# Two side steps of a hand-planned timeline stand later: the queries' transposes of group 0 and the statistics of the first routing

## The chip, the cores and the metric

The kernel runs on one core of one Trainium2 chip. The metric is the device time of one execution in microseconds (us), median over the runs. All arithmetic is in 32-bit floats.

## What is computed

The input is 16 sequences ("batches" here) of 512 tokens by 128 features. Each goes through six stages, each with a residual; `_L0_ffn_ref`, `_L0_attn_ref` and so on are plain functions of the reference:

```python
x = x + 0.5 * _L0_ffn_ref(_layernorm(x), W, b, V_r, C)          # one 128x128 product with a low-rank correction
x = x + _L0_attn_ref(_layernorm(x), ...)                        # 16 heads of 8; state = q; twice: state = softmax(state k^T) v
x = x + 0.5 * _L0_ffn_ref(_layernorm(x), W, b, V_r, C)          # the same first-kind FFN once more
x = x + 0.5 * _L1_ffn_ref(_layernorm(x), gate_w, w1, w2, w3, w1s, w2s, w3s)   # 8 experts, top 2, and a shared one
x = x + _L1_attn_ref(_layernorm(x), ...)                        # 16 heads of 8, masked softmax attention
x = x + 0.5 * _L1_ffn_ref(_layernorm(x), ...)                   # the experts once more, same weights
```

In the first attention q and k are divided by their norms per head before use. In the expert stage `softmax(x gate_w^T)` gives scores, the best two experts of each token are taken, and each does `silu(x w1) * (x w3)`, then `w2`.

## The kernel before, in words

Every engine plays a list of steps that a planner in the same file, class `Timeline` (from L107), has put in order before the program is built. `timeline()` (L277) gives each step a position in **slots** (one slot is one pair of score matmuls, about 2.1 us); a steady batch takes 96 slots (TURN), and work of about four batches is interleaved. `Timeline.close()` (L121) goes through the slots and places each step at the later of its due position and, where it has `behind=(other, gap)`, the place of the other step plus the gap. Steps in SIDE_EVENTS also need room in the slot's TensorE load (COST; FULL 1.0 for the fillers m_gu and m_down, OVER 1.4 for others) and one of three PSUM "side banks"; what finds none waits for the next slot. Then each engine gets its own list, sorted by place plus a lag of that step on that engine (LAG, L97 to L105; the lag of a step that is not listed is 0):

```python
self.order = {e: sorted(numbered, key=lambda m: (m[0] + lag.get(m[2], 0), m[1])) for e, lag in LAG.items()}
```

`play()` (L512) issues each engine's list in that order. A step waits by semaphores for what it needs, and what stands behind it on its engine waits too. The places set the order only, not a time.

The steps that matter here, b being the batch:

- **st(kind, b, g, i)**, L678: two score matmuls (32 rows by 512) of head group g (four heads) into the two banks B_ST; it waits until ScalarE's exponential (L820) of the st before has read them. Kind S1 and S2 are the first and second step of the first attention, L1 is the second attention. Eight st make one window of a group, and ScalarE's exponential writes probs.
- **pv(kind, b, g, kc)**, L693: the products of probs with the values, eight records in the trace. ScalarE or VectorE then copies the result to uts (L832, L1039).
- **sm(kind, b, g, half, tc)**, L714: two score matmuls the other way round (L726), into one pair of banks B_SM, which VectorE reduces to the row maxima (L1072). Each sm waits for the reduction of the one before.
- **p0_op(b, g, i)**, L669: turns the operands of the first attention for head group g, four transposes at L589: i = 0 the keys (stack0k), i = 1 the queries (stack0q). It waits for GpSimd's `low_parts` (L1245: a subtraction at L1248 and a copy at L1250). ScalarE copies the result to kT or qT (L785; in the lag table 1.2 for p0_op, 0.8 for st). The window S1 of group 0 of that batch starts some 8 slots later.
- **ffn_y(b, k)**, L638, the product of the first-kind FFN; k = 1 is the second FFN. VectorE adds it to the tokens in two halves (ffn_y and ffn_rest, both at L951), waits for itself and then raises ffn_done at L961.
- **m_stats(b, k)**, L1090: VectorE's statistics (L920) for the layer norm ahead of the experts; k = 0 is the first of the two expert stages ("routing"). **m_aggr** (L1094): four aggregates (L927) and two small operations (L932, L913), then on GpSimd twelve small operations, Newton's steps for the inverse root (L1177 to L1182; lag 0.6 on GpSimd). **m_xt** (L737): four transposes of the tokens (L589), which wait for ffn_done; ScalarE copies them to xT_m (L785). **m_logits** (L741, VectorE L1097 to L1106): the gate product; on VectorE it waits first for Newton's steps.
- **m_xe(b, k, e)**, L1302 (L1310) on GpSimd: the input of expert e; from the third on it waits until TensorE has done the second half of m_gu for expert e - 2. **m_gu(b, k, e, h)**, L754 (L761) on TensorE: the two products of an expert for half the tokens; ScalarE's tanh (L850) and VectorE's two operations (m_gu L1135, m_up L1141) finish them. At the place of the change, in batch b's first routing, the experts of batch b - 3's second stage are under way.

Of the kernel before, what the change touches and what calls it, by code (L numbers as in the profile page):

```python
# [218 lines left out]
def window(t, start, kind, b, g):  # L219
    for i in range(WIN):  # L220
        t.at(start + i, "st", kind, b, g, i)
    for kc in range(TC):
        t.at(start + 2 * kc + PV_AT, "pv", kind, b, g, kc)
    t.at(start + 10.2, "uts", kind, b, g)
    if kind == "S1":
        t.at(start + DIVIDE_AT, "divide", b, g)
        t.at(start + STATE_AT, "state", b, g)
    else:
        t.at(start + 11.2, "turn", kind, b, g)


def max_job(t, start, kind, b, g):
    seen = [0, 0]
    for slot in SM_AT:

        half = (start + slot + 1) % 2
        t.at(start + slot + 0.01, "sm", kind, b, g, half, seen[half])
        seen[half] += 1
    t.at(start + JOB + 0.6, "mx", kind, b, g)
    t.at(start + JOB + 1.2, "rows", kind, b, g)  # L240


def ffn_events(t, start, b, k):
    t.at(start, "ffn_stats", b, k, behind=(("o_y", b, 0), 1) if k else None)
    t.at(start + 1, "ffn_aggr", b, k, behind=(("ffn_stats", b, k), 1))
    t.at(start + 1.4, "ffn_xt", b, k, behind=(("ffn_stats", b, k), 0.2))
    t.at(start + 2.4, "ffn_bias", b, k, behind=(("ffn_xt", b, k), 0.8))
    t.at(start + 4.2, "ffn_y", b, k, behind=(("ffn_xt", b, k), 1.6))
    t.at(start + 5.2, "ffn_rest", b, k, behind=(("ffn_y", b, k), 1))


def moe_events(t, start, units, unit, b, k):

    t.at(start, "m_stats", b, k, behind=(("o_y", b, 1), 1) if k else (("ffn_y", b, 1), 2))
    t.at(start + 1, "m_aggr", b, k, behind=(("m_stats", b, k), 1))
    t.at(start + 1.4, "m_xt", b, k, behind=(("m_stats", b, k), 0.2))
    t.at(start + 3.8, "m_logits", b, k, behind=(("m_xt", b, k), 1.8))
    t.at(start + 5.2, "m_probs", b, k, behind=(("m_logits", b, k), 1.2))
    t.at(start + 6.6, "m_index", b, k, behind=(("m_probs", b, k), 0.9))
    t.at(start + 6.6 + 1, "m_pick", b, k, behind=(("m_index", b, k), 1))  # L260
    t.at(start + 9.2, "m_gt", b, k, behind=(("m_pick", b, k), 1.3))
    for e in range(EX):
        t.at(units + 2 * unit * e - 2, "m_xe", b, k, e, 
             behind=(("m_gu", b, k, e - 2, 1), 0.8) if e >= 2 else (("m_gt", b, k), 3.5))
        for h in range(2):
            t.at(units + unit * (2 * e + h) + 0.5, "m_gu", b, k, e, h,
                 behind=(("m_xe", b, k, e), 1.2) if h == 0 else (("m_gu", b, k, e, 0), 0.4))
            t.at(units + unit * (2 * e + h) + 0.5 + UP_BEHIND, "m_up", b, k, e, h, behind=(("m_gu", b, k, e, h), UP_BEHIND))
    last = ("m_gu", b, k, NE, 1), 2.2
    for tc in range(TC):  # L270
        for part in range(2):
            t.at(units + 2 * unit * EX + 1.4 + 2 * tc + part, "m_down", b, k, tc, part, behind=last)
            last = ("m_down", b, k, tc, part), 0.4
    return units + 2 * unit * EX + 10


def timeline():  # L277
    t = Timeline()
    for i, at in enumerate(FOLD_AT):
        t.at(at, "fold", i)  # L280
    t.at(MASKS_AT, "masks")
    for b in range(NB):
        t0, t1, t2, t3 = STARTS[b:b + 4]
        early, last = b < EARLY, b == NB - 1
        t.at(t0 - 60 if b else FOLD_AT[0], "load", b, behind=(("store", b - NX), 0.1) if b >= NX else None)
        ffn_events(t, t0 + FFN0_AT, b, 0)
        p = t0 + P0_AT
        t.at(p, "p0_stats", b, behind=(("ffn_y", b, 0), 2))
        t.at(p + 1, "p0_aggr", b, behind=(("p0_stats", b), 1))
        t.at(p + 1.4, "p0_xt", b, behind=(("p0_stats", b), 0.2))  # L290
        t.at(p + 4, "p0_res", b, behind=(("p0_xt", b), 1.4))
        for tc in range(TC):
            t.at(p + 4.6 + tc, "p0_qkv", b, tc, behind=(("p0_xt", b), 2.4))
        t.at(p + 9.4, "p0_squares", b, behind=(("p0_qkv", b, TC - 1), 1.4))
        t.at(p + 11.5, "p0_sums", b, behind=(("p0_squares", b), 1.8))
        for i in range(2):
            t.at(p + 17 + i, "p0_hi", b, i, behind=(("p0_sums", b), 5 + i))
        for g, at in enumerate(P0_OP_AT):
            for i in range(2):
                t.at(t0 + at + i + 0.4, "p0_op", b, g, i, behind=(("p0_hi", b, i), 2.4))  # L300
        for g in range(NG):
            window(t, t0 + (EARLY_S1_AT if early else S1_AT)[g], "S1", b, g)
            window(t, t0 + (EARLY_S2_AT if early else S2_AT)[g], "S2", b, g)
            max_job(t, t0 + (EARLY_MAX_AT if early else S2_MAX_AT)[g], "S2", b, g)
            at = L1_END[b][g] if b in L1_END else t2 + L1_AT[g]
            window(t, at, "L1", b, g)
            max_job(t, at - L1_MAX_END if b in L1_END else t2 + L1_MAX_AT[g], "L1", b, g)
        o = t1 + O0_AT
        t.at(o + 0.4, "o_t", b, 0, behind=(("turn", "S2", b, NG - 1), 1.2))
        t.at(o + 1.9, "o_y", b, 0, behind=(("o_t", b, 0), 1.4))  # L310
        ffn_events(t, o + 3.2, b, 1)
        units, unit, p = (MOE0_END, UNIT_END, P1_END) if last else (t1 + MOE0_AT, UNIT0, t1 + P1_AT)
        if b == 0:
            units, unit, p = t1 + EARLY_MOE0_AT, EARLY_UNIT, t1 + EARLY_P1_AT
        moe_events(t, o + 8.5, units, unit, b, 0)
        done = ("m_down", b, 0, TC - 1, 1), 1.4
        t.at(p, "p1_stats", b, behind=done)
        t.at(p + 1, "p1_aggr", b, behind=(("p1_stats", b), 1))
        t.at(p + 1.4, "p1_xt", b, behind=(("p1_stats", b), 0.2))
        t.at(p + 2.4, "p1_res", b, behind=(("p1_xt", b), 0.8))  # L320
        for tc in range(TC):
            t.at(p + 4.2 + tc, "p1_qkv", b, tc, behind=(("p1_xt", b), 2.4))
        t.at(p + 8, "p1_values", b, behind=(("p1_qkv", b, TC - 1), 0.8))
        for i in range(2):
            t.at(p + 8.2 + i, "p1_hi", b, i, behind=(("p1_qkv", b, TC - 1), 1 + i))
            for n in range(TC):
                t.at(p + 11.4 + 4 * i + n, "p1_op", b, n, i, behind=(("p1_hi", b, i), 3))
        o = OUT1_END.get(b, t2 + O1_AT)
        t.at(o + 0.4, "o_t", b, 1, behind=(("turn", "L1", b, NG - 1), 1.2))
        t.at(o + 1.9, "o_y", b, 1, behind=(("o_t", b, 1), 1.4))  # L330
        units, unit = (MOE1_END[b], UNIT_END) if b in MOE1_END else (t3 + MOE1_AT, UNIT1)
        end = moe_events(t, max(o + 3.2, units - 18), units, unit, b, 1)
        t.at(end, "store", b, behind=(("m_down", b, 1, TC - 1, 1), 1.5))
    return t.close()
# [6 lines left out]
def build(nc, x, ffn_wT, ffn_vT, ffn_cT, ffn_b, wqkv0, bqkv0, wo0, bo0, lnw, lnb,  # L341
          wqkv1, bqkv1, wo1, bo1, src, tgt, gateT, w13, w2, ident, consts, out):
    line = timeline()
    order, no, use = line.order, line.no, line.use
    with ExitStack() as ctx:
# [1018 lines left out]
```

## Time and profile before

| | |
|---|---|
| median of 3 runs | 3438.26 us (3430.40 to 3438.31) |
| profiled execution, its own time | 3441.13 us |
| its span | 3439.3 us |
| mean granted TensorE clock | 0.975 |
| TensorE matmuls busy | 92% of the span |
| VectorE, ScalarE, GpSimd busy | 69%, 60%, 37% |

The rows come from one profiled execution. A busy share is the time in which an engine has an instruction under way. In the timeline a row is one instruction, or several alike that follow each other (x4): its start and length in us, engine, line, operation, what it writes and reads with the shape of each, and in brackets how long the engine had stood still before it and what released it. A matmul in 32-bit floats leaves two records (x8 for pv), one of the scores leaves one. A granted clock of 1.00 is 2.4 GHz, one of 0.50 is 1.2 GHz.

### The profile page before, as it was taken

Reading aid. Unit: us, or ns where it says so; the run is one execution under the profiler, and the core shown is the slowest. Engines: PE = TensorE matmul, PEld = TensorE weight load, DVE = VectorE, ACT = ScalarE, POOL = GpSimd, SP = SyncE. Lnnn points to the kernel's source line nnn. Section 1 sums busy time; section 2 is a strip of 40 time slices with the busy share of each in tenths; the row PEclk is TensorE's granted clock in tenths of the full one; section 3 lists DMA queues with packets and bytes.
Section 4 is the critical chain, followed back from the end, with each engine's and each line's share of the span. In section 5 each row is a group of like instructions: output and inputs, shape, how many; then the busy total and the mean of one; then the engine's idle time right before and its main releaser. Section 6 shows DMA issues by size and latency. Waiting matters only on the chain.

```text
span 3439.3 us, 55298 instructions
## 1 busy us (share of the span) xinstructions
PE 3175.8 (92%) x19942; PEld 1653.5 (48%) x19942; DVE 2360.7 (69%) x5153; ACT 2078.9 (60%) x2689; POOL 1267.5 (37%) x2419
## 2 busy tenths in 40 slices
PE   6898999999999999999999999999999999998899
PEld 3444444444544444454444445444444544444557
DVE  3654675867678686767868676786867677676573
ACT  3464566666656666665666666666666656665442
POOL 3324242343435234243523424352343435223321
PEclk8998999999999999999999999999999999999999
DMA  1000001001100010111010011100101111000111
GB/s 42 4 29 4 32 2 32 32 5 35 32 35 31 31 35 5 35 32 35 30 32 26 14 35 33 35 31 31 35 5 35 32 35 32 30 32 4 60 35 35
DMA packets 81502, 96.89 MB, mean 28 GB/s; under 512 B 50544, under 2 KB 68400, under 8 KB 81104
## 3 DMA queue, kind: packets, MB, share of 16 engines
q1 hardware_dynamic: 81232, 93.35, 8.5%
q8 instruction: 162, 2.65, 0.3%
q14 instruction: 108, 0.88, 0.1%
HBM read 82.76 MB, written 4.78 MB: 25 GB/s over the span
## 4 chain that ended last, share of the span: by engine, by line
PE 62%; ACT 15%; DVE 14%; POOL 5%; issue 4%; ACTq 0%; DMA 0%; SPq 0%; DVEq 0%; POOLq 0%
PE ps L689 16%; PE ps L706 14%; ACT probs L820 13%; PE ps L771 8%; PE ps L761 8%; DVE negmax L1072 6%; PE ps L589 5%; PE ps L726 4%; PE ps L595 2%; PE ps L584 2%; PE ps L654 1%; DVE hid L1141 1%; DVE th L1135 1%; DVE uts L1039 1%; DVE X L951 1%
## 5 line engine op out<-in xcount | busy, mean ns | idle before, releaser
L820 ACT ACTIVATE probs<-ps 128x1024 f32<-128x1024 f32 x1536 | 1574.8, 1025 | 1006.6 <-PE ps L689 991.2
L1072 DVE TENSOR_REDUCE negmax<-ps 128x2 f32<-128x1024 f32 x1024 | 1250.5, 1221 | 452.8 <-PE ps L726 434.8
L689 PE MATMUL ps<-qT,kT 32*128 32x512 f32 x3072 | 779.3, 503 | 117.4 <-ACT probs L820 72.4
L706 PE MATMUL ps<-probs,v 128*32 128x512 f32 x6144 | 839.0, 619 | 0.0
L1310 POOL TENSOR_TENSOR xe<-xT_m,G 128x512 f32<-128x512 f32 x288 | 367.6, 1277 | 988.5 <-PE ps L761 943.6
L761 PE MATMUL ps<-xe,w_sb 128*128 128x256 f32 x2304 | 656.9, 410 | 12.9 <-DVE hid L1141 8.8
L689 PEld LDWEIGHTS ps<-qT,kT 32*128 32x128 f32 x3072 | 289.1, 184 | 768.8 <-ACT probs L820 509.4
L726 PE MATMUL ps<-kT,qT 32*128 32x512 f32 x2048 | 521.4, 504 | 55.0 <-DVE negmax L1072 54.6
L761 PEld LDWEIGHTS ps<-xe,w_sb 128*128 128x128 f32 x2304 | 400.2, 193 | 185.6 <-issue 133.1
L1135 DVE SCALAR_TENSOR_TENSOR th<-th,ps 128x256 f32<-128x256 f32 x576 | 236.4, 411 | 187.3 <-ACT th L850 181.8
L850 ACT ACTIVATE th<-ps 128x256 f32<-128x256 f32 x576 | 221.5, 385 | 149.5 <-PE ps L761 135.5
L771 PEld LDWEIGHTS ps<-w_sb,hid 128*128 128x128 f32 x2304 | 270.0, 191 | 74.5 <-issue 68.5
L771 PE MATMUL ps<-w_sb,hid 128*128 128x128 f32 x2304 | 301.8, 282 | 0.8 <-DVE X L1149 0.5
L1287 POOL TENSOR_TENSOR qT<-maxrow,qT 128x512 fp32r<-128x512 f32 x128 | 163.2, 1275 | 319.8 <-DMA maxrow<-negmaxT 319.8
L1141 DVE TENSOR_TENSOR hid<-ps,th 128x256 f32<-128x256 f32 x576 | 242.3, 421 | 15.5
L726 PEld LDWEIGHTS ps<-kT,qT 32*128 32x128 f32 x2048 | 194.6, 184 | 118.2 <-DVE negmax L1072 60.6
L706 PEld LDWEIGHTS ps<-probs,v 128*32 128x32 f32 x6144 | 122.4, 109 | 192.1 <-issue 187.7
L832 ACT ACTIVATE uts<-ps 128x512 f32<-128x512 f32 x128 | 105.3, 823 | 51.9 <-PE ps L706 48.8
L584 PE MATMUL ps<-id_sb 128*128 128x128 f32 x848 | 124.8, 292 | 0.0
L584 PEld LDWEIGHTS ps<-id_sb 128*128 128x128 f32 x848 | 106.6, 197 | 25.2 <-issue 24.7
L1275 POOL CAST qstack<-st 128x256 fp32r<-128x256 f32 x64 | 25.3, 396 | 217.4 <-DVE st L1045 217.4
L589 PEld LDWEIGHTS ps<-id_sb,uts 128*128 128x128 f32 x512 | 53.9, 140 | 94.8 <-issue 94.3
(171 smaller groups left out, 2684.2 us busy)
## 6 DMA issues: line engine op xcount, KB each, us to landing
G<-gates_dram SPq DMA_DIRECT2D x96, 768.0 KB, 6.2
maxrow<-negmaxT SPq DMA_DIRECT2D x512, 2.0 KB
v<-v_tok SPq DMA_DIRECT2D x256, 18.0 KB, 1.9
X<-in_x SPq DMA_DIRECT2D x16, 256.0 KB, 2.8
out<-X SPq DMA_DIRECT2D x16, 256.0 KB, 2.3
w_sb<-in_w SPq DMA_DIRECT2D x1, 1152.0 KB, 7.1
w_sb<-in_w SPq DMA_DIRECT2D x1, 576.0 KB, 8.7
gates_dram<-gT SPq DMA_DIRECT2D x32, 18.0 KB
```

What stands on the lines that cost most here:

```text
L584: nc.tensor.matmul(bank[:, c * P:(c + 1) * P], id_sb[:], id_sb[:], start=True, stop=True)
L589: ins = nc.tensor.transpose(bank[:, i * P:(i + 1) * P], t, id_sb[:])
L689: nc.tensor.matmul(ps[:, B_ST + h, :], kT[a][rows, g * S + kc * P:g * S + (kc + 1) * P], qT[a][rows, g * S:(g + 1) * S], start=True, stop= ...
L706: ins = nc.tensor.matmul(ps[ROWS * j:ROWS * (j + 1), B_UT, :], v[:, at:at + ROWS], probs[:, n % QUADS, j, :], start=(kc == 0), stop=(kc == ...
L726: nc.tensor.matmul(ps[:, B_SM + h, :], qT[a][rows, g * S + tc * P:g * S + (tc + 1) * P], kT[a][rows, g * S:(g + 1) * S], start=True, stop= ...
L761: ins = nc.tensor.matmul(bank[:, HALF * i:HALF * (i + 1)], w13_sb[:, e, i, :], source, start=True, stop=True)
L771: ins = nc.tensor.matmul(side_bank(key)[:, 0:P], hid[:, e, tc * P:(tc + 1) * P], w2_sb[:, e, :], start=(e == 0), stop=(e == EX - 1))
L820: nc.scalar.activation(probs[:, quad % QUADS, j:j + 2, :], ps[:, B_ST:B_ST + 2, :], ACT.Exp).then_inc(sem["exp_done"], 1)
L1072: nc.vector.tensor_reduce(negative[:, tc, 2 * half:2 * half + 2], ps[:, B_SM:B_SM + 2, :], AX_X, ALU.max, negate=True).then_inc(sem["sm_re ...
L1135: nc.vector.scalar_tensor_tensor(out=th[n % 2][:], in0=th[n % 2][:], scalar=1.0, in1=side_bank(key)[:, 0:HALF], op0=ALU.add, op1=ALU.mult) ...
L1141: nc.vector.tensor_tensor(hid[:, e, HALF * h:HALF * (h + 1)], side_bank(key)[:, HALF:S], th[n % 2][:], ALU.mult).then_inc(read_signal(key), 1)
L1310: nc.gpsimd.tensor_tensor(xe[n % 2][:], xT_m[run % 2][:], G[:, e * S:(e + 1) * S], ALU.mult).then_inc(sem["m_xe"], 1)
```

## The change

It changes two numbers of the timeline. In the first routing of each batch (k = 0) m_stats stands at least 2.9 slots behind the second FFN's ffn_y, where it stood 2 behind; m_aggr and m_xt are tied to m_stats. The queries' p0_op of group 0 is due 2 slots later than before; those of the other groups and all keys' stay.

```diff
 def moe_events(t, start, units, unit, b, k):
 
-    t.at(start, "m_stats", b, k, behind=(("o_y", b, 1), 1) if k else (("ffn_y", b, 1), 2))
+    t.at(start, "m_stats", b, k, behind=(("o_y", b, 1), 1) if k else (("ffn_y", b, 1), 2.9))
     t.at(start + 1, "m_aggr", b, k, behind=(("m_stats", b, k), 1))
     t.at(start + 1.4, "m_xt", b, k, behind=(("m_stats", b, k), 0.2))
...
         for g, at in enumerate(P0_OP_AT):
             for i in range(2):
-                t.at(t0 + at + i + 0.4, "p0_op", b, g, i, behind=(("p0_hi", b, i), 2.4))
+                t.at(t0 + at + i + (2.4 if i and g == 0 else 0.4), "p0_op", b, g, i, behind=(("p0_hi", b, i), 2.4))
```

## Rows read from the trace of the kernel before

**Rows 1.** The chain that ended last, by engine, share of the span.
```profile
PE 62%; ACT 15%; DVE 14%; POOL 5%; issue 4%; ACTq 0%; DMA 0%; SPq 0%; DVEq 0%; POOLq 0%
```

**Rows 2.** TensorE's waits: waiting line, what released it, us in total, times, longest.
```profile
PE ps L589 <- DVEq L961: 18.8, 13, 1.5
PE ps L589 <- POOL stack0q L1250: 14.4, 13, 1.2
```

**Rows 3.** Timeline of TensorE around the queries' transposes of batch 8, start and length.
```profile
1515.28 1.07 PE L706 MATMUL ps<-probs,v 128*32 128x512 f32 x8
1517.45 0.66 PE L589 MATMUL ps<-id_sb,stack0q 128*128 128x128 f32 x4 [1.10 <-POOL stack0q L1250]
...
1518.46 1.16 PE L595 MATMUL ps<-wo,xT_b 128*128 128x128 f32 x8
1519.73 0.50 PE L689 MATMUL ps<-qT,kT 32*128 32x512 f32 x2
```

**Rows 4.** Timeline of GpSimd at the same place.
```profile
1516.59 0.81 POOL L1250 COPY stack0q<-stack0q 128x512 f32<-128x512 f32 x1
```

**Rows 5.** Timeline of ScalarE at the same place.
```profile
1515.41 1.02 ACT L820 ACTIVATE probs<-ps 128x1024 f32<-128x1024 f32 x1 [0.24 <-PE ps L689]
...
1519.58 0.59 ACT L785 ACTIVATE qT<-ps 128x512 fp32r<-128x512 f32 x1
...
1521.36 0.60 ACT L832 ACTIVATE uts<-ps 128x512 f32<-128x512 f32 x1
1522.37 1.02 ACT L820 ACTIVATE probs<-ps 128x1024 f32<-128x1024 f32 x1 [0.41 <-PE ps L689]
```

**Rows 6.** Timeline of TensorE around m_xt of batch 9, at full clock.
```profile
1967.13 1.13 PE L761 MATMUL ps<-xe,w_sb 128*128 128x256 f32 x4
1969.70 0.66 PE L589 MATMUL ps<-id_sb,X 128*128 128x128 f32 x4 [1.44 <-DVEq L961]
...
1970.72 1.07 PE L706 MATMUL ps<-probs,v 128*32 128x512 f32 x8
1972.12 0.50 PE L689 MATMUL ps<-qT,kT 32*128 32x512 f32 x2 [0.33 <-ACT probs L820]
...
1972.55 1.13 PE L761 MATMUL ps<-xe,w_sb 128*128 128x256 f32 x4
...
1980.66 0.50 PE L726 MATMUL ps<-kT,qT 32*128 32x512 f32 x2 [0.38 <-DVE negmax L1072]
```

**Rows 7.** Timeline of GpSimd at the same place: Newton's steps, then m_xe.
```profile
1971.51 0.20 POOL L1179 TENSOR_TENSOR m_n<-m_n 128x4 f32<-128x4 f32 x1 [4.34 <-DVE m_n L913]
...
1974.58 0.20 POOL L1182 TENSOR_TENSOR m_n<-m_n 128x4 f32<-128x4 f32 x1
1974.73 1.27 POOL L1310 TENSOR_TENSOR xe<-xT_m,G 128x512 f32<-128x512 f32 x1
```

**Rows 8.** Timeline of VectorE at the same place.
```profile
1968.99 0.60 DVE L951 SCALAR_TENSOR_TENSOR X<-ps,f_n,X 128x128 f32<-128x128 f32 x2
...
1971.79 0.42 DVE L1141 TENSOR_TENSOR hid<-ps,th 128x256 f32<-128x256 f32 x1
1972.72 1.23 DVE L1072 TENSOR_REDUCE negmax<-ps 128x2 f32<-128x1024 f32 x1 [0.51 <-PE ps L726]
...
1976.60 0.19 DVE L1102 TENSOR_TENSOR lg<-ps,m_n 128x32 f32<-128x32 f32 x1 [0.47 <-PE ps L595]
```

**Rows 9.** Stretches of whole rounds: length; busy us (instructions) per engine; granted clock; DMA share; GB/s.
```profile
929.55:1937.41 1007.86, 947.87 (x5961) 479.17 (x5961) 734.38 (x1600) 648.15 (x841) 393.55 (x750) 0.97 0.09 29
1937.41:2933.18 995.77, 934.13 (x5962) 475.66 (x5961) 733.61 (x1600) 647.76 (x841) 393.51 (x750) 0.99 0.09 29
2534.43:2732.82 198.39, 185.70 (x1193) 94.57 (x1192) 146.70 (x320) 129.51 (x169) 78.73 (x150) 1.00 0.09 30
```

## The prediction

> **What bounds the kernel now.** I read the chain of work that ended last first: 62% of the span is TensorE's, and VectorE, ScalarE and GpSimd share most of the rest [rows 1]. So TensorE's instruction stream sets the time; another engine counts only where TensorE stands still for it. The waits of TensorE come second [rows 2]: 13 waits for a result of the FFN (the VectorE semaphore step at L961), 18.8 us, and 13 for the query operands stack0q from GpSimd, 14.4 us. In the timeline twelve of each lie in the steady rounds (a round is one batch, 96 slots, some 200 us): 1.44 us ahead of the transposes of m_xt for batches 3 to 14, and 1.10 us ahead of p0_op(b, 0, 1) for batches 4 to 15. These are the two steps that the diff moves. Then I read the timeline around one of each, on every engine, because a queue is played in a fixed order: a step that moves passes others on TensorE and, by its lag, on ScalarE, VectorE and GpSimd too. Last came the rounds and their granted clock.
>
> **The query operands, second line of the diff.** By the code, p0_op(8, 0, 1) has stood at slot 719.84; its new due time puts it at 720.7, behind st(S2, 7, 3, 0) at 720 and behind o_y(5, 1), ahead of the st at 721. Nothing is added or removed. On ScalarE its copy (lag 1.2) stood at 721.04 and now stands at 721.9, behind the exponential of the st at 721 (lag 0.8, 721.8) and ahead of the uts copy at 722.2. VectorE, GpSimd and SP keep their order: p0_op has no step on them, and the DMAs of the rows are not passed.
>
> Before: TensorE ends pv at 1515.28 + 1.07 = 1516.35 and then waits until GpSimd's copy of stack0q ends at 1516.59 + 0.81 = 1517.40 [rows 3, 4]. After: the st goes as soon as the exponential before it is read, 1515.41 + 1.02 = 1516.43 [rows 5], so at about 1516.48 to 1516.98; o_y takes 1.16 less the overlap of 0.07, to 1518.08; stack0q has been ready since 1517.40, so the four transposes run without a wait, 0.66 less 0.07, to 1518.67. The next st, at 1519.73 before, starts at 1518.60: its exponential (from 1517.1, 1.02 long) is over by 1518.13. That is **1.13 us** less. Its wait of 1.10 is gone and 0.6 us of cover stands ahead of the same copy.
>
> Does something behind it take this back? ScalarE now runs exponential, copy 0.59, uts 0.60 in a row: from 1519.17, ends at about 1520.20, 1520.7 and 1521.2. The next exponential would be ready at 1522.37 - 1.13 = 1521.24 [rows 5]. So the cover is there, but with 0.05 us only. What ScalarE loses there, 0 to 0.59 (one whole copy), is the bound of this cost; I take 0, as the order just fits. The three side banks are handed out anew for o_y and this step; by the code each takes a bank whose reader has been done for at least 1 us. Twelve rounds by 1.13 is **13.6 us**; the bounds are 12 x 0.54 = 6.5 and 13.6. For batches 0 to 3 the step stood where nothing waits behind it, or keeps its order: 0.
>
> **The routing, first line of the diff.** For batch 9 m_stats goes from slot 934.69 to 935.59, m_xt from 934.9 to 935.79: behind the st at 935 and the pv at 935.6. m_aggr is tied to m_stats + 1 and goes to 936.59: on VectorE behind m_up at 936.42, and on GpSimd (lag 0.6, 937.19) behind m_xe for expert 7 at 937.02. On ScalarE the exponential goes ahead of the copy of xT_m. No DMA is passed.
>
> TensorE first. It is free at 1967.13 + 1.13 = 1968.26 and waits until 1969.70 for the second FFN, whose last VectorE row ends at 1968.99 + 0.60 = 1969.59 [rows 6, 8]. Now st and pv (0.50 and 1.07 less overlaps) fill 1968.2 to 1969.7, m_xt comes at 1969.7 as before, and the next st and sm start at 1970.3 in place of 1972.12: 1.8 us earlier. But the sm behind them waits for VectorE, which has the same work in another order and is through with m_stats, m_gu, m_up and m_aggr at 1971.79 + 0.42 = 1972.21 either way; its reduction then starts 0.5 us earlier than at present, no more. So 1.8 becomes 0.59 by the sm of slot 937.
>
> Then m_logits. VectorE's step waits for the twelve GpSimd instructions of Newton's steps. They ran from 1971.51 to 1974.78, 3.27 us, with 1.8 us to spare before VectorE used them at 1976.60 [rows 7, 8]. Now m_xe stands before them, and m_xe waits for m_gu of expert 5. That ended at 1972.55 + 1.13 = 1973.68 and ends at 1971.85 in the new order; m_xe runs 1.27, so Newton's steps start at 1973.15 and end at 1976.42, and VectorE goes on at 1976.46: **0.14 us** earlier than before. From there VectorE is full to the sm of slot 940, for which TensorE already stands still 0.38 us [rows 6]; TensorE meets it 0.14 us earlier and waits longer. So of 1.44 us removed 0.14 is left, times 12 is **1.7 us**. Bounds: 0, where m_xe ends 0.14 us later than I have it, and 0.59 x 12 = 7.1, where Newton's steps were not late. I take 0.14: it is the sum of measured durations in the order that the code gives. In the trace GpSimd does keep its order: m_xe had its input at 1973.68 and yet started at 1974.73, right behind Newton's last row [rows 6, 7].
>
> The Trainium skill says the same of queues ("Perfetto Trace Analysis", Tensor Engine Instruction: ScalarE, VectorE and GpSimd are strictly first in, first out), and this rule speaks against this part of the change: by it the part gives 1.7 us in all, without it it would give 7.1. The trace agrees with the rule, with the 1.05 us of the row just named.
>
> **The clock.** Ten rounds in a row took 1007.86 + 995.77 = 2003.6 us, mean 200.36; the shortest of them took 198.39, at a granted clock of 1.00 [rows 9]. The first five have 201.57 on average at a mean grant of 0.97: a part of each ran at 1.2 in place of 2.4 GHz, which costs 3.18 us over the shortest round. The other five have 199.15, that is 0.76 over it. So the clock costs 1.97 us a round, and the same work at a given place pays it or not. A round that is 1.27 us shorter need not come back to the same falls each time, which would give up to 1.2 us a round (1.97 less 0.76); against this, the idle time of the routing is not gone but stands later, next to waits that are already there. Bounds: 1.2 x 12 = 14 us of gain, and 15 us of loss, where all twelve rounds are of the long kind (12 x 3.2 = 38 against 12 x 1.97 = 24). I take 4 us of gain, a quarter of the better bound.
>
> **Sum.** 13.6 + 1.7 + 4 = 19.3 us. The profiled execution took 3441.13 (span 3439.3), 2.9 us over the median of the three runs; against it the sum gives 3421.8, against the median of 3438.26 it gives **3419**, which I forecast.
>
> **Rivals.** (1) The routing gives more than I have, 0.59 us or up to 1.44 a round, since Newton's steps are in time or VectorE's slack is larger. For it: 1.8 us of slack before. Against it: the count above. It gives 5 to 15 us more, 3404 to 3414. Chance 0.13. (2) What the query operands give is taken back in ScalarE's row of four, or by the next wait for GpSimd; then 0 to 6 us remain of 13.6, and with the clock's 4 the time is some 3429 to 3434. For it: a cover of only 0.05 us. Chance 0.11. (3) The falls of the clock come in all rounds: 15 us of loss against 15.3 of gain, 3438. Chance 0.10. (4) Slower: the wait of the routing, now moved next to the waits at slots 940 and 941, brings one more fall in each round. One fall cost up to 3.2 / 2 = 1.6 us a round (half of a long round's surplus, an estimate). With all rounds long (15 us) and one more fall in each (19 us) against 15.3 of gain the kernel is 19 us slower, 3457; it decides from the point where rounds lose over 4.1 us each to the clock, against 1.97 now. The five long rounds lost 3.2 on average. Chance 0.06. Beside it the Trainium skill ("TensorE: Matmul & The Clock Gate", What's actually happening) says that the low clock is the default and that activity lifts it; by this rule idle time that is merely moved can move the fall with it. (5) The change doesn't do what it says, since the planner puts the steps back by other rules: worked through in the code it doesn't, chance 0.02. My own case has 0.58.
>
> **Range and chances.** About 0.3%, 10 us, is what a measurement of this kernel can tell from no change. My case with the clock at its two bounds reaches from 3409 to 3438; with part of rival 1 below, 3406, and rival 2 above, 3434, it leaves out most of rivals 3 and 4 and the lower half of 1. Faster by over 0.3%: my case and rival 1 = 0.71; within 0.3%: rivals 2, 3 and 5 = 0.23; slower 0.06.
>
> **What would show it.** Right: no wait of TensorE for stack0q in the rounds; the wait at L961 near 0.1; new waits of TensorE for VectorE of some 0.9 us ahead of the sm of slot 937 and 0.9 ahead of that of slot 940 (0.38 before); GpSimd's m_xe ahead of Newton's steps, and VectorE's m_logits released by them; the shortest round at full clock 197.1 us. Wrong: a shortest round of 198.4 (rival 2) or under 196.7 (rival 1), or a mean granted clock in the rounds under 0.97 (rivals 3 and 4).

## The result, and the profile after

The changed kernel takes **3421.54 us** (median of 8 runs, 3416.62 to 3426.41), the kernel before 3435.85 in the runs beside it. The ratio is 0.9962, 95% interval 0.9946 to 0.9978: 0.38% faster, 13 us by the ratio (7.6 to 18.6). One of the eight executions of the kernel before took 4435.23 us in a slow state; it counts in the median, which is 3433.43 without it, and not in the ratio. The forecast was 3419. The profiled execution took 3423.68 us, span 3421.9, mean granted clock 0.972 (0.975 before).

TensorE's waits, as in [rows 2]. Of the thirteen waits each for L961 and stack0q one of each is left, both in the first 700 us: 1.2 us for stack0q, and for L961

```profile
PE ps L589 <- DVEq L961: 1.6, 1, 1.6
```

Timeline of TensorE at the queries' transposes of batch 8, as in [rows 3]:

```profile
1506.32 1.07 PE L706 MATMUL ps<-probs,v 128*32 128x512 f32 x8
1507.63 0.50 PE L689 MATMUL ps<-qT,kT 32*128 32x512 f32 x2 [0.24 <-ACT probs L820]
1508.06 1.16 PE L595 MATMUL ps<-wo,xT_b 128*128 128x128 f32 x8
1509.05 0.60 PE L589 MATMUL ps<-id_sb,stack0q 128*128 128x128 f32 x4
1509.58 0.50 PE L689 MATMUL ps<-qT,kT 32*128 32x512 f32 x2
```

From the pv to the second st it took 4.45 us (1515.28 to 1519.73) and takes 3.26 (1506.32 to 1509.58). The st, the product and the transposes follow each other with one wait of 0.24 us.

ScalarE at the same place, as in [rows 5]:

```profile
1510.15 1.02 ACT L820 ACTIVATE probs<-ps 128x1024 f32<-128x1024 f32 x1 [0.90 <-PE ps L689]
1511.07 0.59 ACT L785 ACTIVATE qT<-ps 128x512 fp32r<-128x512 f32 x1
1511.55 0.60 ACT L832 ACTIVATE uts<-ps 128x512 f32<-128x512 f32 x1
1512.22 1.03 ACT L820 ACTIVATE probs<-ps 128x1024 f32<-128x1024 f32 x1
```

The row of four is as forecast, and the next exponential starts 0.62 us after the st that it reads (1511.60), as before (1522.37 after 1521.75): the cover just holds.

Timeline of TensorE around m_xt of batch 5, as in [rows 6]. This stretch is at full clock up to 1161.36:

```profile
1154.49 1.06 PE L706 MATMUL ps<-probs,v 128*32 128x512 f32 x8
1155.58 0.66 PE L589 MATMUL ps<-id_sb,X 128*128 128x128 f32 x4
...
1159.14 0.50 PE L726 MATMUL ps<-kT,qT 32*128 32x512 f32 x2 [0.74 <-DVE negmax L1072]
...
1172.42 0.50 PE L726 MATMUL ps<-kT,qT 32*128 32x512 f32 x2 [0.96 <-DVE negmax L1072]
```

Timeline of GpSimd, as in [rows 7]:

```profile
1157.82 1.27 POOL L1310 TENSOR_TENSOR xe<-xT_m,G 128x512 f32<-128x512 f32 x1 [4.78 <-PE ps L761]
1159.05 0.21 POOL L1179 TENSOR_TENSOR m_n<-m_n 128x4 f32<-128x4 f32 x1
...
1162.15 0.20 POOL L1182 TENSOR_TENSOR m_n<-m_n 128x4 f32<-128x4 f32 x1
```

Timeline of VectorE, as in [rows 8]:

```profile
1162.38 0.19 DVE L1102 TENSOR_TENSOR lg<-ps,m_n 128x32 f32<-128x32 f32 x1 [1.11 <-POOL m_n L1182]
```

The reader sees the wait travel. It is gone ahead of m_xt; 0.74 us of it stands ahead of the sm of slot +2 (1159.14), and VectorE then waits 1.11 us for Newton's steps, which stand behind m_xe. At the sm of slot +5 (1172.42) TensorE waits 0.96 us, where it waited 0.38. The forecast had 0.9 at both places. m_logits starts 6.80 us after m_xt, where it was 6.90 (1976.60 less 1969.70): 0.10 us is what is left.

Ten rounds, the first of them (batch 4) and 28.23 us of that round around m_xt; then two stretches, one just ahead of a fall of the clock and one in it. The columns are those of [rows 9]:

```profile
925.68:2918.74 1993.06, 1893.88 (x11922) 962.53 (x11921) 1469.21 (x3200) 1294.14 (x1681) 788.94 (x1500) 0.98 0.09 29
925.68:1123.28 197.60, 188.19 (x1193) 95.67 (x1193) 146.56 (x320) 129.43 (x169) 78.92 (x150) 0.98 0.09 30
950.30:978.53 28.23, 26.00 (x145) 12.34 (x142) 23.99 (x64) 15.54 (x21) 12.85 (x28) 0.88 0.01 2
...
1154.06:1161.36 7.30, 6.37 (x42) 2.94 (x42) 6.33 (x18) 4.26 (x6) 2.88 (x10) 1.00 0.00 0
...
1161.36:1168.19 6.83, 6.83 (x26) 3.00 (x26) 5.28 (x26) 2.81 (x5) 1.59 (x6) 0.50 0.00 0
```

The ten rounds are only 10.6 us shorter (2003.6 before), though the queries alone should give 11.3. The kernel before had rounds at full clock; here **every round from batch 3 to 14 spends 6.8 to 13.7 us in all at the low clock**, and each has a low stretch that begins 5 to 14 us behind m_xt, as the one above at 1161.36, 5.8 us behind it.

What a low stretch costs depends on where it stands. The round above has 6.8 us of it, from 5.4 us behind m_xt on, and takes 197.60 us, only 0.5 us over the 197.1 forecast for full clock. In the kernel before, the round of batch 13 has the same 6.8 us from 14.4 us behind m_xt on and takes 200.36, which is 1.97 over its full-clock round of 198.39. A reading of this, which no run tests by itself: just behind m_xt TensorE would stand still for VectorE anyway, so being slow costs little there.

### The profile page after: what moved, and what is told of

Read it like the earlier page. It is cut to its first block, busy times and chain, and to the rows that moved or that the text cites. A ratio compares the mean times of both kernels' runs of the same rounds, so it can differ in the third digit from the quotient of the medians.

```text
span 3421.9 us, 55298 instructions
## 1 busy us (share of the span) xinstructions
PE 3183.4 (93%) x19942; PEld 1659.5 (48%) x19942; DVE 2362.8 (69%) x5153; ACT 2076.4 (61%) x2689; POOL 1271.0 (37%) x2419
## 4 chain that ended last, share of the span: by engine, by line
PE 62%; ACT 15%; DVE 14%; issue 4%; POOL 4%; ACTq 0%; DMA 0%; SPq 0%; DVEq 0%; POOLq 0%
PE ps L689 16%; PE ps L706 14%; ACT probs L820 13%; PE ps L761 9%; PE ps L771 8%; DVE negmax L1072 6%; PE ps L589 5%; PE ps L726 4%; PE ps L595 2%; PE ps L654 2%; PE ps L584 2%; DVE th L1135 1%; DVE uts L1039 1%; DVE hid L1141 1%; ACT uts L832 1%
```

## The experiments

All times are medians; each ratio is to the kernel before in the same comparison. There the kernel before took 3432.72 us for q_alone to aggr_first, 3433.50 for fill_both to fill_q, 3435.67 for the four fill3 and 3438.83 for fill_xt. A **full-clock round** is the shortest of the rounds of batches 3 to 13 in which the granted clock never fell; the **second eighth** is slots 12 to 24 of such a round, the stretch that holds m_xt and m_logits. The last three columns come from one profiled execution of each kernel, and executions of one kernel differ in their clock (3422.0 us at a mean grant of 0.984 to 3440.9 at 0.975 for the kernel before), so the counts of rounds are rough.

| kernel | us | ratio, 95% interval | full-clock round | its second eighth | rounds without a fall, of 11 |
|---|---|---|---|---|---|
| before | 3435.85 | | 198.39 | 27.73 | 2 |
| both parts (the change) | 3421.54 | 0.9962, 0.9946 to 0.9978 | none | none | 0 |
| q_alone | 3413.64 | 0.9944, 0.9924 to 0.9965 | 197.23 | 27.73 | 2 |
| r_alone | 3438.61 | 1.0020, 1.0006 to 1.0034 | none | none | 0 |
| newton_first | 3406.91 | 0.9928, 0.9909 to 0.9947 | none | none | 0 |
| aggr_first | 3411.33 | 0.9948, 0.9928 to 0.9969 | 196.56 | 27.11 | 1 |
| fill_both | 3410.23 | 0.9935, 0.9917 to 0.9954 | 197.39 | 28.07 | 2 |
| fill_newton | 3402.88 | 0.9911, 0.9895 to 0.9927 | 196.65 | 27.21 | 4 |
| fill_q | 3405.41 | 0.9923, 0.9907 to 0.9939 | 197.00 | 27.73 | 7 |
| fill3_before | 3415.59 | 0.9943, 0.9926 to 0.9960 | 198.14 | 27.72 | 7 |
| fill3_r | 3416.78 | 0.9949, 0.9932 to 0.9966 | 198.13 | 27.63 | 8 |
| fill3_both | 3408.03 | 0.9923, 0.9905 to 0.9941 | 196.82 | 27.61 | 6 |
| fill3_newton | 3409.79 | 0.9921, 0.9903 to 0.9939 | 196.54 | 27.19 | 4 |
| fill_xt | 3404.83 | 0.9913, 0.9892 to 0.9934 | 196.52 | 27.21 | 6 |

### q_alone: the queries' part by itself

```diff
-                t.at(t0 + at + i + 0.4, "p0_op", b, g, i, behind=(("p0_hi", b, i), 2.4))
+                t.at(t0 + at + i + (2.4 if i and g == 0 else 0.4), "p0_op", b, g, i, behind=(("p0_hi", b, i), 2.4))
```

> The queries' part alone. Theory 1 (the two parts add up): the twelve waits for stack0q are gone, a steady round is 1.13 us shorter outside the clock's falls, 13.6 us in all: 3422 us against 3436 before (the medians of eight runs), and the m_xt wait of 1.44 us is still there. Theory 2 (the routing's part costs more through the clock than it gives): this kernel is as fast as the one with both parts, or faster: 3412 to 3421, with falls of the clock no more frequent than before, while the kernel with both parts has 6.8 to 13.7 us at the low clock in every round. Theory 3 (ScalarE's row of four takes it back): 3428 or more.

Measured 3413.64, in theory 2's range. A full-clock round and its second eighth, stretches of the profile:

```profile
2113.33:2310.56 197.23, 185.53 (x1194) 94.63 (x1194) 146.76 (x320) 129.43 (x169) 78.92 (x150) 1.00 0.09 30
2137.95:2165.68 27.73, 23.30 (x145) 11.24 (x141) 24.20 (x64) 15.55 (x21) 12.91 (x28) 1.00 0.01 2
```

The round is 1.16 us shorter than the 198.39 of before [rows 9], against 1.13 forecast, and the second eighth is unchanged. Twelve rounds give 13.9 us; the ratio gives 19 (0.56%). Theory 1 is right on the round, theory 2 on the time. The rest, 5 us, lies within the interval's 7 us either way, so the times do not show that the clock gained anything here. The grants point that way: their mean is 0.983 over the 7 executions, against 0.980 over 18 of the kernel before, where 0.001 of grant went with about 2.1 us (18.9 us over 0.009). Theory 3 is out.

### r_alone: the routing's part by itself

```diff
-    t.at(start, "m_stats", b, k, behind=(("o_y", b, 1), 1) if k else (("ffn_y", b, 1), 2))
+    t.at(start, "m_stats", b, k, behind=(("o_y", b, 1), 1) if k else (("ffn_y", b, 1), 2.9))
```

> The routing's part alone. Theory 1: 0.10 to 0.14 us a round, 1.7 us: 3434 us. Theory 2: the idle time that is moved behind m_xt makes the clock fall in every round in the stretch from 5 to 14 us behind m_xt, which costs more than 0.14: 3436 to 3450, mean granted clock in the rounds 0.965 or less. Outside the falls both expect the same: no wait at m_xt, 0.74 us ahead of the sm of slot +2, m_logits released on VectorE by Newton's last step.

Measured 3438.61, ratio 1.0020, and the interval leaves out 1: **by itself this part makes the kernel slower**, by 7 us, though every wait that it moves is as counted. No round is free of falls, as theory 2 has it; but the mean grant of the rounds is 0.98, not its 0.965 or less. Over all executions the mean grant is 0.973 (12 of them), against 0.980 (18) for the kernel before. In the profile the round of batch 5 takes 198.80 us, with 6.8 us at the low clock from 5.4 us behind m_xt on, and those with 10.2 us take 200.5 to 201.4. The two ratios multiply to 0.9964, and the change has 0.9962: the parts add up.

### newton_first and aggr_first: who takes the routing's gain

newton_first changes GpSimd's order alone, in the steady rounds; aggr_first puts m_aggr back on VectorE as well, so that against the kernel before only TensorE's and ScalarE's order is changed at this place.

```diff
# newton_first, on top of the change
-             "rows": 2 * HOP, "divide": 1.0},
+             "rows": 2 * HOP, "divide": 1.0, "m_aggr": 0.4},
```

```diff
# aggr_first, on top of the change
-    t.at(start + 1, "m_aggr", b, k, behind=(("m_stats", b, k), 1))
+    t.at(start + (1 if k else 0), "m_aggr", b, k, behind=(("m_stats", b, k), 1 if k else 0.2))
```

> Both parts, and on GpSimd alone m_aggr's Newton steps stand ahead of m_xe again (lag 0.4 in place of 0.6). If m_xe ahead of them is what holds the routing's gain down to 0.1 us (theory 1), VectorE's m_logits starts some 0.45 us earlier behind m_xt than with both parts, released by TensorE's product (at 6.3 to 6.4 us behind m_xt instead of 6.8), and the kernel is 5.4 us faster than with both parts: 3416. If VectorE is full anyway (rival), m_logits comes earlier but the sm of slot +5 does not, and the time stays at 3421.

> Both parts, with m_aggr right behind m_stats on VectorE as in the kernel before, and so Newton's steps ahead of m_xe on GpSimd too. Theory 1: the same gain as with the lag alone, 3416, since VectorE has the same work up to the next reduction either way. Rival: the order on VectorE is what counts, and this one is faster or slower than the other by over 3 us.

VectorE's first step of m_logits and TensorE's m_xt in newton_first, batch 5, two timelines:

```profile
1158.48 0.19 DVE L1102 TENSOR_TENSOR lg<-ps,m_n 128x32 f32<-128x32 f32 x1 [0.49 <-PE ps L595]
```

```profile
1152.30 0.66 PE L589 MATMUL ps<-id_sb,X 128*128 128x128 f32 x4
```

The step comes 6.18 us behind m_xt and is released by TensorE's product, no longer by Newton's steps. The second eighth at full clock in aggr_first:

```profile
747.44:774.55 27.11, 23.47 (x144) 11.21 (x141) 24.09 (x64) 15.47 (x21) 12.82 (x28) 1.00 0.01 2
```

It is 0.62 us shorter than the 27.73 of before, where the forecast's bound without the queue was 0.59. So TensorE's part of the move is worth 0.6 us a round, and the order on VectorE and GpSimd takes 0.5 of it. The order on GpSimd alone takes 0.4, by the full-clock stretches of fill_newton and fill3_newton below (27.21 and 27.19, against 27.61 of fill3_both). The times went further than the 3416 expected of both: newton_first by 9 us. Its rounds have 5.1 us at the low clock on average, those of the change 9.5. aggr_first is 4.4 us slower than newton_first, over the 3 us of the rival, but the intervals overlap, so a difference by VectorE's order is not shown.

### fill_both, fill_newton, fill_q: extra products that hold the clock

To set the clock apart I gave TensorE redundant work just where it waits; FILL lists the experts and halves.

```diff
+FILL = ((4, 0), (5, 1), (6, 0), (6, 1))
...
                 source = xe[(EX * run + e) % 2][:, HALF * h:HALF * (h + 1)]
+                if k == 1 and b < 12 and (e, h) in FILL:
+                    nc.tensor.matmul(bank[:, 0:HALF], w13_sb[:, e, 0, :], source, start=True, stop=True)
                 for i in range(2):
```

In fill_q, on top of q_alone, (5, 0) stands in place of (5, 1); fill_newton is on top of newton_first.

> Both parts, and in rounds 3 to 14 four extra products of 0.5 us on TensorE (m_gu's first product twice, the first one overwritten), right ahead of the longest waits for VectorE's reductions. If the moved idle time makes the clock fall (theory 2), the falls go, the granted clock in the steady rounds is 0.99 or more, and a round takes 197.1 to 197.5 us: 2 us a round less than the 199.3 of both parts, 3395 to 3402. If the falls have another cause, the clock stays at 0.97 and the four products make the kernel as slow as with both parts or up to 24 us slower: 3421 to 3445.

> The same four products with Newton's steps ahead of m_xe. Without falls a round takes 198.4 - 1.13 - 0.6 = 196.7 us against 197.1 to 197.5 with both parts and the products: the worth of the GpSimd order, free of the clock, is 0.5 us a round, 6 us, and the kernel takes 3390 to 3396. If VectorE is full anyway (rival), it is the same as the kernel with both parts and the products.

> The queries' part alone with four such products (one of them ahead of the m_xt wait of 1.44 us in place of the wait behind it). Without falls a round takes 197.3 us: against the kernel with both parts and the products this gives the routing's part free of the clock, 0.10 us a round or 1.2 us, so 3397 to 3403. If the routing's part lost time by something else than the clock, this kernel is 5 us or more faster than that one.

fill_both missed its time: 3410, not 3395 to 3402. The falls became shorter, 2.7 us a round on average against 9.5, but only two rounds had none. And it carried a cost that I had not counted. GpSimd and VectorE in fill_both behind m_xt of batch 10, which began at 2142.50:

```profile
2145.17 1.27 POOL L1313 TENSOR_TENSOR xe<-xT_m,G 128x512 f32<-128x512 f32 x1 [5.20 <-PE ps L764]
```

```profile
2149.73 0.19 DVE L1105 TENSOR_TENSOR lg<-ps,m_n 128x32 f32<-128x32 f32 x1 [1.54 <-POOL m_n L1185]
```

The product in expert 5 comes ahead of the one for which m_xe waits: m_xe starts 2.67 us behind m_xt (2.24 in the change) and m_logits 7.23 (6.80), both 0.43 later, and the second eighth is 28.07 in place of 27.61. This is the chain m_gu, m_xe, Newton, m_logits seen from the other side: it passes a delay on in full. fill_newton, where the chain is cut, has 27.21 with the same products. It is 7 us faster than fill_both, though the intervals overlap, and its 3403 missed the 3390 to 3396; it too has falls left, in 7 rounds of 11. fill_q's 3405 missed 3397 to 3403. It is 5 us faster than fill_both, which its expectation takes for a sign that the routing loses by something else than the clock; but fill_both's delay of 0.43 us in twelve rounds is 5 us too, so these three do not price the routing by themselves.

### fill3: the same without the product in expert 5

> The kernel before, with three of the extra products (experts 4 first half, 6 both halves; none in the half that m_xe and Newton's steps wait for). It is the ground for the next two. Theory 2: the extra products keep the clock up, so it is as fast as the kernel before or a few us faster though it does more, 3425 to 3436, and a round free of falls takes 198.4 as before. Rival: 0.5 us for each product, 10 to 20 us slower.

> The routing's part alone, with the same three products. A round free of falls takes 198.3 us against 198.4 in the one before: the part gives 0.10 us a round when the clock is left out. Theory 2 (its loss is the clock's): the ratio of this kernel to the kernel before with the products lies under that of the two without products (1.002), at 0.998 to 1.001. Rival (it loses by a wait): rounds free of falls are longer than 198.4.

> Both parts with the three products: rounds free of falls take 197.15 us (the four products took 197.4, since one of them delayed m_xe and with it Newton's steps), and the second eighth of the round 27.63 us against 27.73 before. Time 3403 to 3412. If the product in expert 5 was not what delayed that one, the second eighth stays at 28.07.

> Both parts, Newton's steps ahead of m_xe, three products. Rounds free of falls take 196.6 us, the second eighth 27.1 to 27.2: 0.5 us a round better than fill3_both, 6 us: 3397 to 3405, the fastest so far. If VectorE were full anyway, it would equal fill3_both.

FILL is ((4, 0), (6, 0), (6, 1)) on top of the kernel before, r_alone, the change and newton_first. Second eighths at full clock, fill3_before, then fill3_r:

```profile
1940.00:1967.72 27.72, 24.09 (x148) 12.00 (x145) 24.18 (x64) 15.64 (x21) 12.85 (x28) 1.00 0.01 2
```

```profile
1346.84:1374.47 27.63, 24.37 (x148) 12.01 (x145) 24.00 (x64) 15.60 (x21) 12.85 (x28) 1.00 0.01 2
```

Here is the routing's part free of the clock: 0.09 us in this stretch, in fill3_both 0.11 (27.61). The whole full-clock rounds do not show it: 198.13 against 198.14, where 0.1 less was expected, and their last eighths differ by 0.2 us among rounds of one kernel. They do show that the rival is out, since no round free of falls is longer than 198.4 but one of 198.43 (fill3_before has one of 198.49). In time the two kernels are level, 3416.8 against 3415.6, ratios 0.9949 and 0.9943; this alone does not tell them from a loss of 0.2%, as each interval is 0.17% either way. Together with the rest it points at the clock: r_alone, whose mean grant is lower over all executions, loses 0.2% without a fall-free round, and where 8 and 7 rounds of 11 are free of falls the routing's part loses nothing in them. That it *gains* its 1 us is seen in the stretches only. fill3_before also beats the kernel before by 0.57%, 20 us, more than expected, by doing more. fill3_both came as expected in time (3408) and second eighth (27.61); its shortest round is 196.82, not 197.15. fill3_newton missed: a full-clock round is 0.28 us shorter than in fill3_both, but the two times cannot be told apart.

### fill_xt: work in the wait behind m_xt

```diff
# on top of fill3_newton
+                if k == 0 and 3 <= b < 15:
+                    bank = take_side(("m_xt", b, k))
+                    for i, x_t in enumerate(token_chunks(b)):
+                        nc.tensor.transpose(bank[:, i * P:(i + 1) * P], x_t, id_sb[:])
                 turn_chunks(("m_xt", b, k), token_chunks(b))
```

> The kernel with both parts, Newton's steps ahead of m_xe and three products, and m_xt's four transposes done twice in batches 3 to 14 (0.6 us, the first time overwritten). In its neighbour without this the falls that are left begin 5.3 to 6.6 us behind m_xt, where TensorE waits 1.3 us for VectorE ahead of the sm of slot +2. Theory 2: this wait is the cause, the transposes fill half of it, the falls at that place go, rounds free of falls still take 196.6 us, and the time is 3393 to 3400. Rival: these falls have another cause; then the twelve repeats cost 0 to 7 us: 3406 to 3414.

Measured 3404.83, between the two ranges. The repeats are free at full clock (27.21 against 27.19). Falls that begin 5.3 to 6.6 us behind m_xt went from seven to three in the 11 rounds of the profiled executions, and two longer ones came at 15.6 and 15.7. This is inconclusive on the place of the falls.

## Why the prediction was right, and where not

**The sum and its sign held**; the 19.3 us forecast came out as 13 by the ratio, just outside its 7.6 to 18.6. That 3419 was nonetheless only 2.5 us off is in part luck: the forecast was taken from a median of 3438.26, and in the eight executions beside the change the kernel before had 3435.85. The miss in the gain and that in the ground partly cancel.

**Queries, 1.13 us a round: right.** q_alone shows 1.16, the orders on TensorE and ScalarE are as derived, and the cover of 0.05 us on ScalarE was enough. Rival 2 is out. (Its 3429 to 3434 left out the routing's 1.7 us; with it the same terms give 3427 to 3433.)

**Routing, 0.14 us a round: right in size and mechanism.** Measured 0.09 to 0.12 in the second eighth with the clock out of the way; over a whole round it is too small to be seen. The rule of the queue, with which the part gives 1.7 and without it 7.1, is borne out by newton_first, aggr_first and the kernels on top of newton_first: the second eighth is 0.52 to 0.62 us shorter than before when Newton's steps do not stand behind m_xe. The bound of 0.59 was right, though the rows by it give 0.51 (1972.72 less 1972.21) and the prediction does not say where the rest comes from.

**The clock, a gain of 4 us: wrong, and with the wrong sign for the routing's half.** For the whole change the two orders give 15 us (12 times 1.16 and 0.10) and the ratio 13, so the clock took about 2 us; with the interval it is between 7.5 lost and 3.5 gained, and the forecast 4 lies just outside. The step that failed is "A round that is 1.27 us shorter need not come back to the same falls", where I let the better bound outweigh the sentence behind it, that the idle time "stands later, next to waits that are already there". r_alone measures this at +7 us for the kernel, with about 1 us of gain counted in, so some 8 us of loss (3 to 13 by the interval). For the queries' half the sentence may have held: q_alone's 5 us beyond its order, and its grant, point to a gain. In the change itself rival 3's condition came true, falls in all rounds, but at a small part of its 15 us. Its price took every round for a long one, 3.2 us over full clock; here the rounds with 6.8 us of low clock right behind m_xt lie only 0.5 over it. Nor did its sign of being wrong appear, a mean grant in the rounds under 0.97: it was 0.98. r_alone ends slower, as in rival 4, but not by one more fall in each round: its 11 rounds have 16 falls and 9.6 us at the low clock on average, those of the kernel before 14 and 6.5. The queries' 14 us hid this loss.

What stays open: why a low stretch comes at one place and not at another in the same order of instructions. In these runs more time at the low clock went with the waits moved next to each other, and less with work put in the waits; they give no rule that would tell in which round.

## What to carry to other kernels

Move a step on one engine only after you have looked where it lands in the queues of all the others: here TensorE's half of the move was worth 0.6 us a round, and the same number in the planner put GpSimd's twelve small steps behind a wait that took most of it back. Before you count a removed wait as time, follow the next engine that is nearly full; the wait reappears where TensorE meets it. And where a kernel sits at the edge of TensorE's full clock, price each part alone: two parts with a good sum can hold one that loses.

## What the runs showed of the hardware that I had not expected

Three redundant products of about 0.5 us in each of twelve rounds made the kernel before 0.57% faster (3415.59 against 3435.67, interval 0.40% to 0.74%), with falls in 4 rounds of 11 in place of 9 in the profiled executions, and a mean grant of 0.988 over 5 executions in place of 0.979 over 11. No wait of TensorE in the ten rounds of the kernel before is over 1.5 us, and none over 1 us in those of the change; there TensorE is busy for 6.37 of the 7.30 us ahead of the fall at 1161.36, and still the clock went from 2.4 to 1.2 GHz. Of the versions tried, fill_newton has the lowest ratio, 0.9911 (3402.88 us), which fill_xt's 0.9913 equals within the interval, and without redundant work newton_first, 0.9928 (3406.91). Both are faster than the kernel before; against the change newton_first's interval (up to 0.9947) just touches the change's (from 0.9946).
